# Polynomial attention and mixture of experts on one core: the next batch's q/k/v products inside the attention steps

## What is computed

```python
x = x + attn(layernorm(x))          # x: (4, 512, 512)
# attn: q, k, v = split(x @ w_qkv); q, k = layernorm_of_each_head(rope(q)), same for k
#   a = tril((q @ k.T) ** 4);  out = (a / a.sum(-1)) @ v;  out @ w_out
x = x + moe(layernorm(x))
# moe: scores = sigmoid(x @ gate.T); 2 of 4 groups, then 4 of 16 experts by score + bias
#   weights = 2.5 * chosen scores / their sum
#   sum over the chosen of weight * (silu(x @ g.T) * (x @ u.T)) @ d.T, plus the shared expert
```

## Time and profile before

| what | us |
|---|---|
| median of 3 runs (lowest, highest) | 1266.75 (1262.48, 1269.29) |
| span of the profiled execution | 1278.8 |
| batch 0: attention loop | 76.2 to 150.4 |
| batch 2: products, loop, projection with transposes | 336.3, 396.5, 484.9 to 501.4 |
| batch 3: products, loop | 501.4, 562.0 to 651.3 |
| mixture | 681.3 to 1278.8 |

### The profile page before, as it was taken

How to read it: one execution, slowest core, us unless ns; L and a number is a source line. 1 busy time by engine, 2 the same in 40 slices (tenths; PEclk the granted TensorE clock), 3 DMA queues, 4 the chain that set the end, 5 groups by cost and what they waited for, 6 DMA issues and landing times. The chain is left out here.

```text
span 1278.8 us, 21813 instructions
## 1 busy us (share of the span) xinstructions
PE 1013.0 (79%) x5786; PEld 483.4 (38%) x5787; DVE 782.5 (61%) x1641; ACT 571.1 (45%) x1018; POOL 503.3 (39%) x738
## 2 busy tenths in 40 slices
PE   5956799666997669976588889888888888878893
PEld 2422245222444214442145445344344344434341
DVE  2855578587695885858955866444544545544442
ACT  2377624767147672366735324333333333323330
POOL 0047500556003751026631102555555555555552
PEclk9977898677996689967787889999999999989997
DMA  8015430144501438104445786777877778877774
GB/s 323 1 50 188 159 131 1 50 149 146 183 3 49 140 107 327 69 0 148 148 149 178 264 321 216 188 171 178 187 185 179 170 177 191 192 154 183 169 178 77
DMA packets 76782, 194.36 MB, mean 152 GB/s; under 512 B 9920, under 2 KB 11072, under 8 KB 75328
## 3 DMA queue, kind: packets, MB, share of 16 engines
q1 hardware_dynamic: 58816, 150.58, 34.5%
q0 software_dynamic: 17920, 43.26, 18.9%
HBM read 132.72 MB, written 61.10 MB: 152 GB/s over the span
## 5 line engine op out<-in xcount | busy, mean ns | idle before, releaser
L606 PE MATMUL bank<-arena,xgT 128*128 (+1 forms) x1152 | 287.4, 387 | 4.0 <-ACT xgT L817 3.1
L853 POOL TENSOR_TENSOR s_p<-s_p,c_causal 128x128 f32<-128x128 f32 x256 | 128.8, 530 | 400.0 <-DVE s_p L1193 397.6
L552 PE MATMUL bank<-s_p,vtok 128*32 128x128 f32 (+3 forms) x512 | 118.0, 605 | 95.9 <-DVE arena L1143 49.5
L810 ACT ACTIVATE hT<-bank 128x512 f16<-128x512 f16 x96 | 57.3, 597 | 276.5 <-PE bank L616 264.6
L462 PE MATMUL bank<-arena 128*128 128x512 f32 x384 | 168.6, 597 | 2.0 <-issue 2.0
L606 PEld LDWEIGHTS bank<-arena,xgT 128*128 128x128 f16 x1152 | 109.6, 100 | 133.5 <-issue 44.4
L627 PE MATMUL bank<-wd,hT 128*128 128x512 f16 x576 | 152.7, 405 | 0.7 <-ACT hT L810 0.7
L898 POOL DMA_INDIRECT out<-yy,sidx x80 | 128.4, 1605 | 45.7 <-issue 44.7
L861 POOL TENSOR_TENSOR arena<-arena 128x768 f16<-128x768 f32 x68 | 115.7, 1702 | 71.9 <-ACT arena L684 71.5
L817 ACT ACTIVATE xgT<-bank 128x1024 f16<-128x1024 f16 x96 | 98.2, 1023 | 90.7 <-PE bank L597 89.1
L1367 DVE TENSOR_SCALAR yy<-bank,hsc 128x512 f32<-128x512 f32 x80 | 60.0, 750 | 125.8 <-DMA out<-yy,sidx 106.6
(11 more groups left out here) (155 smaller groups left out, 1453.3 us busy)
## 6 DMA issues: line engine op xcount, KB each, us to landing
wd<-w_scratch SPq DMA_DIRECT2D x82, 512.0 KB
arena<-w_experts SPq DMA_DIRECT2D x34, 768.0 KB, 5.9
w_scratch<-arena SPq DMA_DIRECT2D x34, 768.0 KB, 4.5
arena<-w_scratch SPq DMA_DIRECT2D x17, 1024.0 KB, 8.0
xin<-x SPq DMA_DIRECT2D x5, 1024.0 KB, 9.1
arena<-x SPq DMA_DIRECT2D x4, 1024.0 KB, 7.1
x_scratch<-arena SPq DMA_DIRECT2D x4, 1024.0 KB, 4.5
xn_scratch<-vtok SPq DMA_DIRECT2D x4, 1024.0 KB, 5.0
```

The costliest lines, as they stand in the source:

```text
L552: mm = pe.matmul(bank[6 + n][r, P * kb:N], w, s_p4[:, (i - 1) % 2, j, 0:N - P * kb], start=(kb == 0), stop=(kb == MB - 1), skip_group_chec ...
L606: mm = pe.matmul(bank[2 + k][:], xgT[:, k, xh * EC + c, :], w, start=(c == 0 and xh + wh == 0), stop=(c == EC - 1 and xh == 1))
L853: pool.tensor_tensor(d, d, C["causal"][:], ALU.mult).then_inc(p4_masked, 1)
```

## The change

Buffers. q16, k16, vtok and attT exist twice and are taken by `b % 2`; the temporaries of the products (`t1`, `t2`, `qk32`) have room of their own. To find it, wqkv, one attT and one k16 lie where the five early experts go. `xn2` and its transposed copy lie over `xres`. q16 shares its room with attT.

Order. `sequence(b)` is written out for all four batches on all engines. The products of batch b + 1 are done in the steps of batch b (`fill`), one of q, k, v in a step, in banks 4 and 5, with DVE's and ACT's part in `ahead`. The second norm, its transposes, logits and routing of batch b - 1, and the first norm and transposes of batch b + 2, are in the same steps (`fill_behind`, `behind`). Batch 3 has no products and takes only routing (`last_fill`, `last_behind`). The transposes of x after the last batch are gone. Batch 0's products run ahead as before, with the first norm and transposes of batch 1 added.

Group end. `finish` transposes bank 7 in blocks of 32x32, takes the reciprocal of one element of each block column (128x16), transposes it back with a stride of zero, and multiplies.

SP. The loads of the five early experts move from behind batch 2's halves to ahead of batch 3's, with a wait for batch 2's projection; the store of xn16, the reload of xres and the store of the weights stand between weight halves.

```diff
-        wqkv = over([EC, 3 * E])
+        wqkv = low(0, EC * 3 * E).rearrange("p (a b) -> p a b", a=EC)
+        attT = [low(3, NG * N).rearrange("p (a b) -> p a b", a=NG), over([NG, N])]
+        q16 = [split16(a) for a in attT]
...
+                if b == B - 1:
+
+                    sp.wait_ge(proj_ps, MB * (B - 1))
                     for j in range(2):
                         sp.wait_ge(halves_out[j], 16 * EARLY)
                     for e in range(EARLY):
                         load_expert(e)
+                halves_of(b, 0, 2)
+                if b:
+                    sp.wait_ge(xn16_ready, b)
...
+            def fill(b, i):
...
+                if i % MB == 0:
+                    if i == 0 and b >= 2:
+                        table(b - 2, bkB)
+                    if m:
...
+                        qk_transposes(nb, m - 1, bkA, bkB)
+                elif i % MB == 1:
+                    if m:
+                        pe.wait_ge(qkT_sb, 2 * upto(nb, m - 1) - 1)
+                    qkv(nb, m, 0, bkA, q_ps)
+                elif i % MB == 2:
...
+                    elif i == 14 and b:
+                        pe.wait_ge(places_here, b)
+                    if m:
+                        pe.wait_ge(qkT_sb, 2 * upto(nb, m - 1))
+                    qkv(nb, m, 1, bkB, k_ps)
+                elif m:
...
+                    qkv(nb, m, 2, bkA, v_ps)
...
+                for i in range(NG * MB):
+                    scores(b, i)
+                    if nb < B and i % MB:
+                        fill(b, i)
+                    if i:
+                        values(b, i - 1)
+                    if nb < B and i % MB == 0:
+                        fill(b, i)
+                    if nb < B:
+                        fill_behind(b, i)
...
+                values(b, NG * MB - 1)
+                if nb < B:
+                    pe.wait_ge(v_sb, upto(nb, 3))
+                    if lb < B:
+                        pe.wait_ge(xT_sb, upto(lb, 3))
+                    qk_transposes(nb, 3, bkA, bkB)
...
+                projection(b)
...
             def finish(b, g):
+
+                blocks = lambda a: a.rearrange("p (c i) -> p c i", i=D)
+                a = attT[b % 2][:, g, :]
                 dve.wait_ge(pv_done, b * (NG * MB) + (g * MB + MB))
-                dve.reciprocal(rec, bank[7][:])
-                dve.drain()
-                dve.tensor_tensor(attT[:, g, :], bank[6][:], rec, ALU.mult).then_inc(att_done, 1)
+                dve.transpose(a, bank[7][:])
+                dve.drain()
+                dve.reciprocal(inv[:], blocks(a)[:, :, 0])
+                dve.drain()
+                dve.transpose(blocks(a), inv[:].unsqueeze(2).to_broadcast([P, N // D, D]))
+                dve.drain()
+                dve.tensor_tensor(a, bank[6][:], a, ALU.mult).then_inc(att_done, 1)
...
+            def ahead(b, i):
+
+                nb, m = b + 1, i // MB
+                if i % MB == 0:
+                    if m:
+                        head_variance(nb, m - 1)
+                elif i % MB == 1:
+                    if m:
+                        finish(b, m - 1)
+                        split_qk(nb, m - 1)
+                elif i % MB == 2:
+                    rope_q(nb, m, bkA)
+                else:
+                    rope_k(nb, m, bkB)
+                    centre(nb, m)
+
+            def behind(b, i):
...
+                if i % MB == 0 and i:
+                    head_normed(nb, i // MB - 1)
...
+                if i == 0:
+                    row_stats()
+                elif i == 1:
+                    if b >= 2:
+                        add_table(b - 2, bkB)
+                    row_normed(pb)
+                elif i == 2:
+                    rows_lo(pb)
+                elif i == 8:
+                    group_sums(pb)
+                elif i == 9:
+                    group_choice()
+                elif i == 10:
+                    compare(mb[:], NX)
+                elif i == 12:
+                    expert_choice()
+                elif i == 13:
+                    choice_weights(pb)
+                elif i == 14:
+                    choice_values()
+                    choice_places(pb, bkB)
+                elif i == 15:
+                    place_rows(0)
...
+                    if nb < B:
+                        ahead(b, i)
+                        fourths(b, i)
+                        behind(b, i)
```

More of the change, by code:

```diff
@@ L862, in split_lo @@
                                    ).then_inc(lo_done, 1)
-            sequence(0)
-            with pool.Fori(0, B - 1) as r:
-                sequence(r + 1)
+            for b in range(B):
+                sequence(b)
             for i in range(4):
```

774 lines of the change are left out of this document (489 added, 285 removed).

## The result

| | kernel before | changed kernel |
|---|---|---|
| median of its runs, us | 1268.02 (1262.48 to 1273.07, 4 runs) | 1224.51 (1220.50 to 1227.54, 4 runs) |
| last projection begins | 651.28 | 604.57 |
| first gate/up product of the mixture | 684.25 | 638.18 |

The ratio is 0.9651, with a 95% interval of [0.9615, 0.9687]: faster. The prediction had 1219 us in a range from 1186 to 1250. The profiled execution took 1220.5 us, 1218.5 of them span.

What follows compares the result with a forecast made beforehand. No single engine bounds the loop, but a ring of PE, ACT, DVE and POOL waiting for each other. First fourths, loops, tails and 8 us contention end the last table at about 603, before 651.3; gain 47, 1219 us, range 1186 to 1250.

Steps and rivals of the forecast that it cites:

- The step cost: Merged loops: each interval between fourths takes its most loaded engine's time, scaled by 0.98; loops 0 to 2 98, 122.5, 121.5 us.
- the clock: Loops 1 and 2: PE's granted clock should be above 0.75.
- The group end: DVE's finish: two transposes at 0.69, small reciprocal, product and drains, about 2.4 us in place of 4.1.
- The tails: Last fourths of a batch to the next batch's first: 28 us, with projection 14.0 and eight hand-overs of 0.2.
- Batch 3: Last loop, without products: ACT's work plus row work, logits and ranks, 83 us scaled, plus 5 for last values and table.
- PE's wait at group ends gone: Sign in the loops: PE no longer waits at group ends, the finish standing ahead of the next step's own fourths.
- Contention: Moved DVE operations now beside POOL: 0.2 us for each of 20 a loop, 8 us together; wrong if moved sums average over 1.4.
- exclusive lock: Shared SBUF access blocks the loser for the whole instruction; estimated 6 us a loop, time near 1229.
- A: Rival, chance 0.25: engines run a step ahead, heavy DVE and ACT intervals pair up in the loops; 33 us less, 1186.
- B: Rival, chance 0.12: longer copy, product, rope chains, one product at half rate on the path in about 11 groups; 38 us, 1257.
- C: Rival, 0.05 together with a slow transpose: PE's queue closes the ring over all engines; slower above 4.4 us a group, 1293.
- D: Rival, chance 0.05: the loop stretches by all it takes in and the time stays, 1263 us.

Runs made afterwards that it cites:

- e3: Changed kernel with one of four chunks of the logits' product, so routing scores use a quarter of each row; 1207.5 us, ratio 0.9532 to the kernel before.
- e11: Kernel of e7 with e8's group ends, batch 3's logits made two blocks each in steps 4 and 5; 1201.5 us, ratio 0.9486 to the kernel before.
- e12: Kernel of e7 with e8's group ends, the last loop's logits all in step 4 and what follows one step earlier; 1195.2 us, ratio 0.947.
- e8: Changed kernel, in batch 3 the group end put behind the fourths of the next group's first step; 1225.6 us, ratio 0.9676 to the kernel before.
- e4: Changed kernel with POOL's low halves of the expert weights cut to a sixteenth, the rest zero; 1193.1 us, ratio 0.942 to the kernel before.
- e6: Changed kernel reordered: last loop's logits in steps 5 and 6, step 8 head squares before logits' copy, step 14 places before q's rope; 1219.9 us.
- e7: Kernel of e6 with two of the four products of v moved one step later each; 1204.4 us, ratio 0.9529 to the kernel before.

## Why the prediction was right, step by step

| stretch, us | forecast | measured |
|---|---|---|
| first fourths of batch 0 | 80.8 | 81.0 |
| loop 0, fourths to fourths | 98 + 4 contention | 102.9 |
| tail 0 | 28 | 23.5 |
| loop 1 | 122.5 + 2 | 124.8 |
| tail 1 | 28 | 26.3 |
| loop 2 | 121.5 + 2 | 123.9 |
| tail 2 | 28 | 26.3 |
| batch 3 to its table | 88 | 95.9 |
| last projection | about 603 | 604.6 |

A loop here runs from its first fourths (L1418) to its last ones, and a tail from there to the first fourths of the next batch.

**The step cost** held as a sum: three loops within 1 us. Its single intervals did not. Between the starts of the fourths in loop 0 the third interval of a group, taken at 6.9 us, took 8.7, 9.1, 8.9 and 8.7, which is 35.3 in all where 4 x 6.9 x 0.98 is 27.0. In the two middle groups the first took 10.7 (for 9.9, with the norm statistics) and 8.3 (for 8.7), the second 3.4 and 6.7 for 6.2, the fourth 6.6 and 5.3 for 5.1. I had taken the third for DVE's own work alone; DVE also waits in it, for PE's product of k:

```profile
178.41 0.69 DVE L1375 TENSOR_TENSOR arena<-bank,c_rope_cos 128x512 f32<-128x512 f32 x1 [2.25 <-PE bank L484]
```

Of the 8.2 us between these the 4 charged for contention cover half, and shorter second intervals (21.7 for 24.3) a part. That loop 0 came out within 1 us is to that extent luck.

**The period** of loops 1 and 2 came to 151.1 and 150.2, **the clock** to 0.84 and 0.83, DVE to 103.8 us in the loop of batch 1. **The group end** is this in the changed kernel's timeline of DVE, in place of 4.1 us:

```profile
583.88 0.70 DVE L1355 STREAM_TRANSPOSE arena<-bank 128x512 f32<-128x512 f32 x1
584.66 0.25 DVE L1357 RECIPROCAL inv<-arena 128x16 f32<-128x16 f32 x1
584.99 0.71 DVE L1359 STREAM_TRANSPOSE arena<-inv 128x512 f32<-128x512 f32 x1
585.77 0.69 DVE L1361 TENSOR_TENSOR arena<-bank,arena 128x512 f32<-128x512 f32 x1
```

It takes 2.6 us for the 2.4 I had; the transpose is 0.70, taken at 0.69. The Trainium skill ("Vector Engine (DVE) Microarchitecture Reference", The reshape front-end and per-opcode configuration) says that the transpose sustains one element per cycle and lane. The rows agree: 0.70 us for 512 elements a lane, where the product over the same shape takes 0.69.

**The tails** were mis-sized by 1.7 to 4.5 us. Of 28 I had 14.0 for the projection, which took 14.5 to 15.4. Behind it, to the first fourths of the next batch, I had 3.3 and hand-overs; measured 2.1. Ahead of it I had 9.1 and hand-overs; 6.0 measured in tail 0 and 9.7 in the others. So neither the terms nor the hand-overs were as long as I had them. Of the place rows, which I had all under the projection, the first block stands on DVE from 332.5 to 336.7 us, between the last fourths and the sum of the heads' squares; tail 0 has none, and it is the shorter one.

**Batch 3** is the term that failed, 7.9 us short. The three tails were too long by 4.5, 1.7 and 1.7, 7.9 us as well, and the two cancel in the sum. That is luck: no run ties one to the other, and either alone would have put the forecast some 8 us off. I had batch 3 as ACT's work plus row work and a sum for logits and ranks, with nothing for PE's own interval. Two things were missing: the logits run at the low clock there (7.01 us, not 3.75), and they sit ahead of 48.6 us in which DVE, not ACT, sets the pace. e3, e11 and e12 take 3.8, 3.3 and 5.9 us out of this loop by making the logits fewer or earlier; e8 shows that the 17.5 us of PE's wait for the group end, the row that catches the eye, is worth 1.8. "PE's wait at group ends gone" held nearly in loops 1 and 2 (1.2 us each) and not here.

**Contention** was wrong as a mechanism, though the loops with it came out right. I charged 8 us for operations that get POOL as a neighbour. Two of the three kinds that took 1.23 us did get longer: the sum of 128x1024 takes 1.39 us on average and 1.49 in loop 1, the head norm 1.42, and the subtraction of the mean stays at 1.23; together they make 1.34, just under my mark of 1.4. But at the same time the operations that had POOL beside them before got shorter, which fits the same POOL work spread over a longer loop: place rows 613 to 474 ns, all 128 fourths 679 to 601. In net, POOL's low halves, with what they do to the masks, are worth 23.3 us in the changed kernel against 27.2, not 8 more. DVE's busy time of one whole period fell from 124.3 us (batch 2, product stage to projection) to 112.2; the cheaper group end explains 6.8 of that by its rows. The rule I had set against my rows, the Trainium skill's exclusive lock ("SBUF — State Buffer", SBUF: two separate sides), described single operations well: the place row's L1326 takes 273 ns at least, 281 in the median and 1658 at most, as long as POOL's 1708, and at most 500 in e4. As a total the 6 us a loop that I had estimated from it for added contention was wrong too, for the same reason as mine: both counted neighbours gained and not neighbours lost.

**The rivals.** A (smoother) was not seen: no loop came out under its interval sum. (The loops as I listed them give 30 us less than the forecast's and not 33, so A's price was 1189.) B's low clock was right in kind and wrong in size. Besides the logits of the last loop (3.3 us) it is in the k product of step 14 in loops 1 and 2, behind 5.21 us in which PE waited for DVE to read the places:

```profile
319.89 6.75 PE L484 MATMUL bank<-arena 128*128 128x512 f32 x8 [5.21 <-DVE rb L1293]
470.08 6.75 PE L484 MATMUL bank<-arena 128*128 128x512 f32 x8 [5.21 <-DVE rb L1293]
```

At full clock such a product takes 3.70, and DVE's rope waited 4.08 and 3.80 us behind these. In e6, which reads the places ahead of the rope of q, they take 5.33 and 5.40. The q products of the first steps took from 3.70 to 5.40. If the three stood whole on the path, the low clock cost 9.4 us there, an estimate from these rows (3.3 + 2 x 3.05), and not 38, for in the loops with products the granted clock rose. C's ring over PE's queue exists, as e7 shows (10.6 us over three loops for two products moved by a step), but that is 0.9 us a group, against the 4.4 from which it would decide. D fell.

## What to carry to other kernels

When work moves beside a contending engine, sum the contention of both versions whole: an operation gains a neighbour where another loses it. When a step issues a small product behind a lull, price it at the low clock, and look at where it stands in the queue, since a wait named after ACT or DVE can be due to PE's order two steps back. A wait of 17.5 us in a row can be worth 1.8 us of time: before moving anything, ask which engine is busy without a gap at that place, for that engine keeps the time where it is. And when a sum comes out right, compare its terms one by one, for two that are wrong can cancel.

## What the runs showed of the hardware that I had not expected

- A 32x32 block transpose on DVE of 128x512 f32 costs as much as the product over the same shape (0.69), 0.70 us from PSUM and 0.71 from SBUF, while the reciprocal of the same shape costs 3.35. Two transposes and a reciprocal of 128x16 (0.25) are half its price.
- Cutting POOL's low halves (1.71 us each, 68 in all) to a sixteenth took 23 to 27 us out of the time ahead of the last projection in either kernel, by way of DVE's operations, of the masks on POOL, or of both. On DVE it shows on the fourths, the place rows and the sum of 128x1024, and not on two other operations with both inputs in SBUF (L1367, L1397). It comes in large pieces: the sum of 128x1024 takes 1224 ns at least and 1901 at most, but 1227 at most in e4.
- The head norm (L1409, the mean in loop 1) stays at 1412 ns with the low halves cut, where the same operation took 1226 in the product stage of the kernel before. At 105.9 and 164.0 us, where it takes 1.48 and 1.47, masks of POOL run beside it, and at 338.8, where POOL is idle, it takes 1.23; no run isolates the masks.
- The same 32 small matmuls took 3.75 us or 7.01 us according to what PE did ahead of them (busy 9.65 of 10.8 us at a granted clock of 1.00, or in a stretch at 0.50 that began behind 5.0 us with 1.85 busy); splitting them into two groups behind a lull (3.60 each) saved nothing.
